# Self attention of a two-layer block: scores computed in both orientations, no transposed probabilities, the high parts of the exponentials made on ScalarE

## The chip, the cores and the metric

One core of a Trainium2 chip runs the whole program in one launch. The metric is device time in microseconds (us). The engines are TensorE (PE, with its weight loads PEld), VectorE (DVE), ScalarE (ACT), GpSimd (POOL) and SyncE (SP), which here only issues DMAs.

## The reference

The input x is 8 batches of 512 tokens with 512 features, the context 8 batches of 77 tokens with 384. Layer 0 is a cross attention and a feed-forward block, layer 1 a self attention, a cross attention and a feed-forward block. The change touches the self attention alone. In float32:

```python
xn = layernorm(x)                                   # eps 1e-5
q, k, v = (xn @ w.T + b).reshape(8, 512, 16, 32).transpose(0, 2, 1, 3)   # each with its own w, b
p = softmax(q @ k.T * 32 ** -0.5, axis=-1)          # 512 x 512 for each of 8 x 16 heads
x = x + (p @ v).transpose(0, 2, 1, 3).reshape(8, 512, 512) @ wo.T + bo
```

## The kernel before

The program runs five phases one after the other, with a barrier between them: L0ca, L0ff, L1sa, L1ca, L1ff. `self_attention` (line 525) is L1sa. Every matmul operand is split in two: a high part, rounded to the type fp32r, and a low part, what is left. A product takes three matmuls, high by high, low by high and high by low (`product`, line 88). High parts are made by ACT (`add_hi`, line 94), low parts by DVE (`add_lo`, line 100), those of the normalised tokens hT by POOL (`ln_lo`, line 231).

Per batch there are projections q and k in 4 groups of 4 heads each, V and the output O in 4 token tiles each (4 quarters each, a quarter is one `product` of 512 columns, 3 matmuls), and T, which transposes the normalised tokens (4 blocks of 4 transpositions). For the scores SP copies q and k into stacks (`stacks`, line 589): the 128 rows of the contraction hold the parts of one head as (high, high, low, low) of q against (high, low, high, low) of k, so one matmul gives the whole product (`scores`, line 700). A group takes 16 DMAs.

A batch is 64 steps v; a head is 4 of them. The order of the work is written out by hand in tables of steps (lines 575 to 580, `T_STEPS` and so on), the same on each engine. In step v, PE makes the scores of a tile six steps ahead, transposes four 128x128 blocks of normalised probabilities Pr (`P_transposed`, line 713) and multiplies V by the transposed probabilities of two steps before (`PV`, line 727; six matmuls of 256 columns). DVE takes the maxima of a score tile (line 934), ACT makes the exponentials with the negative maxima as bias and the row sums as a by-product (line 846), DVE inverts the sums (line 942), POOL multiplies (line 1060). ACT then makes the high part PTh of the transposed block and DVE the low part PTl. V is laid into zeroed blocks (`place_v`, line 1068) so that four heads fill the four quarters of one output bank.

```python
def body(b, last):
    for v in range(TILES):
        ...
        if ahead and v + LEAD != TILES:
            scores(*tile(b, v + LEAD))
        P_transposed(b, v)
        if v >= LAG:
            PV(b, v - LAG)
```

Each engine takes its instructions in order and waits at semaphores; a wait holds all that is queued behind it. A prologue loads the weights through four staging slots, which are the memory of Pr, splits them, normalises the tokens of batch 0 and computes q, k of group 0 and V.

## Time and profile before

| | us |
|---|---|
| median of 3 runs | 3689.26 (3686.32 to 3692.94) |
| the profiled execution | 3688.11, its span 3686.3 |
| PE busy | 3448.7 (94% of the span) |
| DVE, ACT, POOL busy | 1816.3, 1802.7, 1138.8 |
| self attention's window 1318 to 2412 | 1094, of it PE busy 1069.6 |

The span is the time from the first to the last instruction. A matmul's duration in the trace contains its way through the array, so two that follow each other overlap; what one costs is the distance of their starts. The same holds, less so, for ACT and DVE.

### The profile page before, as it was taken

What the parts mean: (1) busy time and instruction counts of PE and PEld (TensorE: products, weight loads), DVE (VectorE), ACT (ScalarE), POOL (GpSimd) and SP (SyncE); (2) the same over time, 40 slices, a digit from 0 to 9 for tenths busy, and PEclk for the clock granted to TensorE, in tenths of its full rate; (3) what the DMA queues carried; (4) which work ended last, traced back from release to release, by engine and by line L of the source; (5) the groups of instructions that cost most, each with busy time, mean ns of one, the idle gap of its engine ahead of it and who ended that gap; (6) DMA issues with size and microseconds to landing.
All of it is one profiled execution on the core that took longest, in us unless ns stands there. A gap on an engine that the chain in (4) does not pass through costs nothing. (4 is left out here: it accounts for less than half of the span.)

```text
span 3686.3 us, 51567 instructions
## 1 busy us (share of the span) xinstructions
PE 3448.7 (94%) x18384; PEld 2905.3 (79%) x18384; DVE 1816.3 (49%) x3472; ACT 1802.7 (49%) x4868; POOL 1138.8 (31%) x1576
## 2 busy tenths in 40 slices
PE   4899979999999799999999999977999989999999
PEld 3788858888888578888888888855888768888887
DVE  3566644222222277777777767745666442222221
ACT  2677634222222266666667667735667542222222
POOL 2455521111111134444434435414455311111110
PEclk8999989999999899999999999988999989999999
DMA  3112123111111232322322332321221131111010
GB/s 95 39 58 71 61 83 99 39 35 35 35 35 35 72 92 72 101 74 75 94 80 69 94 91 59 92 69 53 76 72 48 52 112 52 35 35 35 35 35 35
DMA packets 158341, 232.91 MB, mean 63 GB/s; under 512 B 35894, under 2 KB 53510, under 8 KB 158086
## 3 DMA queue, kind: packets, MB, share of 16 engines
q1 hardware_dynamic: 158086, 229.63, 20.7%
q8 instruction: 146, 2.39, 0.3%
q14 instruction: 109, 0.89, 0.1%
HBM read 115.45 MB, written 41.94 MB: 43 GB/s over the span
## 5 line engine op out<-in xcount | busy, mean ns | idle before, releaser
L1060 POOL TENSOR_SCALAR L1sa_Pr<-L1sa_Pr,L1sa_rinv 128x512 f32<-128x512 f32 x512 | 354.8, 702 | 595.7 <-DVE L1sa_rinv L942 595.7
L102 DVE TENSOR_TENSOR L1sa_PTl<-L1sa_t,L1sa_PTh 128x512 fp32r<-128x512 f32 x512 | 352.2, 688 | 193.2 <-ACT L1sa_PTh L96 183.5
L96 ACT ACTIVATE L1sa_PTh<-L1sa_t 128x512 fp32r<-128x512 f32 x512 | 305.6, 597 | 266.2 <-PE L1sa_o L91 251.2
L846 ACT ACTIVATE L1sa_Pr<-L1sa_s,L1sa_nmax 128x512 f32<-128x512 f32 x512 | 350.9, 685 | 77.8 <-DVE L1sa_nmax L934 72.3
L934 DVE TENSOR_REDUCE L1sa_nmax<-L1sa_s 128x1 f32<-128x512 f32 x512 | 346.9, 678 | 17.7 <-PE L1sa_s L709 17.7
L89 PE MATMUL L1sa_o<-L1sa_PTh,L1sa_Vbh 128*128 128x256 f32 x1024 | 330.4, 323 | 3.5 <-DVE L1sa_oTl L103 2.1
L422 DVE TENSOR_TENSOR L0ff_gl<-L0ff_gf,L0ff_gh 128x512 fp32r<-128x512 f32 x128 | 95.2, 743 | 475.3 <-ACT L0ff_gh L382 475.3
L422 DVE TENSOR_TENSOR L1ff_gl<-L1ff_gf,L1ff_gh 128x512 fp32r<-128x512 f32 x128 | 95.8, 749 | 473.1 <-ACT L1ff_gh L382 473.1
L723 PE MATMUL L1sa_t<-ident,L1sa_Pr 128*128 128x128 f32 x2048 | 312.2, 275 | 14.0 <-DVE L1sa_PTl L102 12.8
L723 PEld LDWEIGHTS L1sa_t<-ident,L1sa_Pr 128*128 128x128 f32 x2048 | 243.5, 141 | 92.8 <-DVE L1sa_PTl L102 24.5
L368 ACT ACTIVATE L0ff_gf<-L0ff_f,cols 128x512 f32<-128x512 f32 x128 | 88.3, 690 | 451.0 <-PE L0ff_f L91 451.0
L368 ACT ACTIVATE L1ff_gf<-L1ff_f,cols 128x512 f32<-128x512 f32 x128 | 88.3, 690 | 449.7 <-PE L1ff_f L91 449.7
L91 PE MATMUL L1sa_o<-L1sa_PTl,L1sa_Vbh 128*128 128x256 f32 x1024 | 288.9, 282 | 0.0
L90 PE MATMUL L1sa_o<-L1sa_PTh,L1sa_Vbl 128*128 128x256 f32 x1024 | 288.4, 282 | 0.0
L709 PE MATMUL L1sa_s<-L1sa_stack_k,L1sa_stack_q 128*128 128x512 f32 x512 | 205.2, 401 | 5.6 <-ACT L1sa_Pr L846 4.0
L89 PE MATMUL L0ff_f<-L0ff_hTh,L0ff_Wh 128*128 128x512 f32 x512 | 203.4, 397 | 5.7 <-POOL L0ff_hTl L232 5.7
L89 PE MATMUL L1ff_f<-L1ff_hTh,L1ff_Wh 128*128 128x512 f32 x512 | 202.9, 396 | 5.7 <-POOL L1ff_hTl L232 5.7
L89 PEld LDWEIGHTS L1sa_o<-L1sa_PTh,L1sa_Vbh 128*128 128x128 f32 x1024 | 194.8, 190 | 7.8 <-DVE L1sa_oTl L103 6.8
L90 PE MATMUL L0ff_f<-L0ff_hTh,L0ff_Wl 128*128 128x512 f32 x512 | 200.6, 392 | 0.0
L91 PE MATMUL L0ff_f<-L0ff_hTl,L0ff_Wh 128*128 128x512 f32 x512 | 200.5, 392 | 0.0
L90 PE MATMUL L1ff_f<-L1ff_hTh,L1ff_Wl 128*128 128x512 f32 x512 | 200.1, 391 | 0.0
L91 PE MATMUL L1ff_f<-L1ff_hTl,L1ff_Wh 128*128 128x512 f32 x512 | 200.0, 391 | 0.0
(296 smaller groups left out, 9380.3 us busy)
## 6 DMA issues: line engine op xcount, KB each, us to landing
L1sa_stack_q<-L1sa_parts_q SPq DMA_DIRECT2D x256, 128.0 KB, 2.7
L1sa_stack_k<-L1sa_parts_k SPq DMA_DIRECT2D x256, 128.0 KB, 2.7
L0ff_xs<-x SPq DMA_DIRECT2D x64, 256.0 KB, 3.5
L1sa_xs<-x SPq DMA_DIRECT2D x64, 256.0 KB, 3.5
L1ff_xs<-x SPq DMA_DIRECT2D x64, 256.0 KB, 3.5
L0ca_xs<-in_x SPq DMA_DIRECT2D x32, 256.0 KB, 3.6
L0ca_stage<-in_x SPq DMA_DIRECT2D x32, 256.0 KB, 3.9
x<-L0ca_stage SPq DMA_DIRECT2D x32, 256.0 KB, 2.0
```

The lines of the kernel that those rows point to most:

```text
L89: nc.tensor.matmul(out, wh, xh, start=first, stop=False)
L90: nc.tensor.matmul(out, wl, xh, start=False, stop=False)
L91: return nc.tensor.matmul(out, wh, xl, start=False, stop=last)
L96: return nc.scalar.activation(hi, bank, ACT.Copy)
L102: return nc.vector.tensor_tensor(lo, bank, f32(hi), ALU.subtract)
L368: nc.scalar.activation(gf[:, j % 2, :], f1_bank[j % 2][:, :], ACT.Gelu, bias=b1[:, j:j + 1])\
L422: nc.vector.tensor_tensor(gl[:, j % 2, :], gf[:, j % 2, :], f32(gh[:, j % 2, :]), ALU.subtract)\
L709: nc.tensor.matmul(s_bank[s % S_BANKS][:, :], stack["q"][:, g % 2, j, qt * P:(qt + 1) * P], stack["k"][:, g % 2, j, :], start=True, stop=T ...
L723: last = nc.tensor.transpose(t_bank[v % 2][:, (2 * k + q) * P:(2 * k + q + 1) * P], Pr[:, h % 2, qt, kt * P:(kt + 1) * P], cst.ident[:, :])
L846: nc.scalar.activation(Pr[:, h % 2, qt, :], s_bank[s % S_BANKS][:, :], ACT.Exp, bias=nmax[:, h % 2, qt:qt + 1], accum_out=rsum[:, h % 2, q ...
L934: nc.vector.reduce_max(nmax[:, h % 2, qt:qt + 1], s_bank[s % S_BANKS][:, :], AX.X, negate=True)\
L1060: nc.gpsimd.tensor_scalar(p, p, rinv[:, h % 2, qt:qt + 1], 0.0, ALU.mult, ALU.add)\
```

## The change

The self attention is rewritten; the other phases are as before.

- A step n is now a pair of tiles (32 steps a batch, 2 a head). The scores are taken in both orientations: query rows by key columns (`scores`), only for the maxima, and key rows by query columns (`scores_T`), for the exponentials. The stacks keep three of the four combinations of parts (96 rows), and two further rows hold the negative maxima, high and low, on q's side and ones on k's. So `scores_T` comes out with the maximum subtracted, and exp has no bias.
- The maxima (DVE) are split by POOL (`m_split`), transposed by PE into the first columns of the bank pair of `scores_T` (`m_transposed`), copied by ACT (`m_copy`) and put into the stack by a DMA (`m_rows`).
- exp writes E, 128x1024. ACT makes its high part Eh by a Copy (`e_hi`, for all steps: `EH_BY`), POOL in even and DVE in odd steps the low part El (`e_lo`). `PV` multiplies them with Vst, whose 96 columns are interleaved: V high, V low and ones, so that the sums come out as the third of three rows. It takes high and low in two halves of the step, 2 matmuls of 512 columns each.
- The result of a head, not normalised (96 rows), is copied out by ACT (`o_out`) and laid side by side by a DMA (`line_up`); per 4 heads POOL adds the two parts, DVE inverts 128x512 sums, POOL multiplies, ACT and DVE split.
- The projections are cut into quarters and spread evenly over the 64 half steps of a batch (`sa_pieces`). The order is q, k of group 2, O of the batch before, q, k of group 3, T, then q, k of group 0, V and q, k of group 1 of the next batch. `evacs[n]` are those whose bank is emptied in step n: T0 in step 15, T1, T2 and T3 in step 16.
- The weights come through three staging slots. The prologue also makes q and k of group 1.

```diff
+SA_ORDER = ([("q", 0, 2), ("k", 0, 2)] + [("O", -1, t) for t in range(TT)] + [("q", 0, 3), ("k", 0, 3)]
+            + [("T", 1, c) for c in range(KT)] + [("q", 1, 0), ("k", 1, 0)] + [("V", 1, t) for t in range(TT)]
+            + [("q", 1, 1), ("k", 1, 1)])
+SA_FIRST = [("T", c) for c in range(KT)] + [("q", 0), ("k", 0)] + [("V", t) for t in range(TT)] + [("q", 1), ("k", 1)]
+STEPS = H * 2
+def sa_pieces():
+    quarters = [(*u, c) for u in SA_ORDER for c in range(1 if u[0] == "T" else KT)]
+    halves = [[] for _ in range(2 * STEPS)]
+    for i, q in enumerate(quarters):
+        halves[i * 2 * STEPS // len(quarters)].append(q)
+    return halves
...
-        stack = {n: ph.sb(f"stack_{n}", [P, 2, 4, S], F32R) for n in "qk"}
+        KD, KM = 3 * HD, 3 * HD + 2
+        stack = {n: ph.sb(f"stack_{n}", [P, 8, S], F32R) for n in "qk"}
         parts = {n: ph.sb(f"parts_{n}", [P, 2, S], F32R) for n in "qk"}
-        Vh, Vl = (ph.sb(n, [P, TT, D], F32R) for n in ("Vh", "Vl"))
-        Vbh, Vbl = (ph.sb(n, [P, TT, 4, P], F32R) for n in ("Vbh", "Vbl"))
-        Pr = ph.sb("Pr", [P, 2, TT, S])
-        PTh, PTl = (ph.sb(n, [P, 2, S], F32R) for n in ("PTh", "PTl"))
-        nmax, rsum, rinv = (ph.sb(n, [P, 2, TT]) for n in ("nmax", "rsum", "rinv"))
+        V = ph.sb("V", [P, TT, 2, D], F32R)
+        VS = 5
+        Vst = ph.sb("Vst", [P, TT, VS, HD, 3], F32R)
+        E = ph.sb("E", [P, 2, 2 * S])
+        Eh, El = ph.sb("Eh", [P, 2, 2 * S], F32R), ph.sb("El", [P, 2, 2 * S], F32R)
+        nmax = ph.sb("nmax", [P, 2, TT])
+        mm = ph.sb("mm", [P, 2, 2 * TT], F32R)
+        mT = ph.sb("mT", [2 * TT, 2, P], F32R)
+        osb = ph.sb("osb", [3 * HD, S])
+        OLN = ph.sb("OLN", [P, 3, S])
+        onorm = x.htmp
...
-        wt = weight_staging(ph, [flat(Pr[:, i // 2, 2 * (i % 2):2 * (i % 2) + 2, :]) for i in range(4)])
+        wt = weight_staging(ph, [E[:, 0, :], E[:, 1, :], flat(OLN[:, 0:2, :])])
...
+        s_bank = ctx.enter_context(nc.psum_tensor(f"{name}_s", [P, 2, S], F32))
+        st_bank = ctx.enter_context(nc.psum_tensor(f"{name}_st", [P, 2, S], F32))
+        o_bank = ph.banks("o", 2)
...
+        LEAD_S, LEAD_T = 6, 2
...
+        EH_BY, EL_BY = ("act", "act", "act", "act"), ("pool", "dve", "pool", "dve")
...
+            def stacks(n, group, pair):
+                pset = 2 * group + pair
+                full = e_stack[pset % 4].sem
+                sp.wait_ge(e_qkl.sem, e_qkl.no(2 * group + "qk".index(n)))
+                if group >= 2:
+                    sp.wait_ge(e_st.sem, e_st.no(8 * (group - 2) + 4 * pair + 3))
+                for j in range(2 * pair, 2 * pair + 2):
+                    src = f32(parts[n][HD * j:HD * (j + 1), :, :])
+                    dst = f32(stack[n][:, 4 * (group % 2) + j, :])
+                    once, twice = (src[:, 0, :], src) if n == "k" else \
+                        (src[:, 1, :], src[:, 0:1, :].broadcast_to([HD, 2, S]))
+                    sp.dma_start(dst[0:2 * HD, :], twice).then_inc(full, 16)
+                    sp.dma_start(dst[2 * HD:3 * HD, :], once).then_inc(full, 16)
+            def m_rows(h):
+                sp.wait_ge(e_mc.sem, e_mc.no(h))
+                sp.dma_start(f32(stack["q"][KD:KM, h % 8, :].rearrange("a (t n) -> a t n", t=TT)),
+                             f32(mT[:, h % 2, :])).then_inc(e_m[h % 2].sem, 16)
+            def line_up(h):
+                sp.wait_ge(e_ob.sem, e_ob.no(h))
+                if h % 4 == 0 and h > 0:
+                    sp.wait_ge(e_on.sem, e_on.no(h // 4 - 1))
+                sp.dma_start(OLN[HD * (h % 4):HD * (h % 4 + 1), :, :],
+                             osb[:, :]).then_inc(e_oln.sem, e_oln.unit)
...
+                    if n % 2 and 0 <= (n + 3) // 2 < HEADS:
+                        m_rows((n + 3) // 2)
+                    if n % 2 == 0 and n >= 2:
+                        line_up((n - 2) // 2)
+                    if n < 0:
+                        continue
+                    for step, kind, ahead, g, pair in ((3, "q", 0, 2, 0), (5, "k", 0, 2, 0), (6, "q", 0, 2, 1),
+                                                       (6, "k", 0, 2, 1), (14, "q", 0, 3, 0), (14, "q", 0, 3, 1),
+                                                       (16, "k", 0, 3, 0), (16, "k", 0, 3, 1), (20, "q", 1, 0, 0),
+                                                       (22, "k", 1, 0, 0), (22, "q", 1, 0, 1), (22, "k", 1, 0, 1),
+                                                       (31, "q", 1, 1, 0), (31, "q", 1, 1, 1), (0, "k", 0, 1, 0),
+                                                       (0, "k", 0, 1, 1)):
+                        if step == s and exists(b + ahead) and not (b == 0 and s == 0):
+                            stacks(kind, (b + ahead) * G + g, pair)
...
+            def scores(n):
+                h, slot = n // 2, n // 2 % 8
+                if n % 4 == 0:
+                    pe.wait_ge(e_stack[n // 4 % 4].sem, e_stack[n // 4 % 4].no(n // 16))
+                if n > 0:
+                    pe.wait_ge(e_mx.sem, e_mx.no(n - 1))
+                for i in range(2):
+                    qt = 2 * (n % 2) + i
+                    last = nc.tensor.matmul(s_bank[:, i, :], stack["q"][0:KD, slot, qt * P:(qt + 1) * P],
+                                            stack["k"][0:KD, slot, :], start=True, stop=True)
+                last.then_inc(e_s.sem, e_s.unit)
+            def scores_T(n):
+                h, slot = n // 2, n // 2 % 8
+                if n % 2 == 0:
+                    pe.wait_ge(e_m[h % 2].sem, e_m[h % 2].no(h // 2))
+                if n % 2 and (n + 1) // 2 < HEADS:
+                    pe.wait_ge(e_mc.sem, e_mc.no((n + 1) // 2))
+                elif n > 0:
+                    pe.wait_ge(e_ex.sem, e_ex.no(n - 1))
+                for i in range(2):
+                    kt = 2 * (n % 2) + i
+                    last = nc.tensor.matmul(st_bank[:, i, :], stack["k"][0:KM, slot, kt * P:(kt + 1) * P],
+                                            stack["q"][0:KM, slot, :], start=True, stop=True)
+                last.then_inc(e_st.sem, e_st.unit)
+            def m_transposed(h):
+                pe.wait_ge(e_mm.sem, e_mm.at(h, 1))
+                if h > 0:
+                    pe.wait_ge(e_ex.sem, e_ex.no(2 * h - 2))
+                nc.tensor.transpose(st_bank[0:2 * TT, 0, 0:P], f32(mm[:, h % 2, :]), cst.ident[:, :])\
+                    .then_inc(e_mt.sem, e_mt.unit)
+            def PV(n, low):
+                h = n // 2
+                if low:
+                    by = EL_BY[n % 4]
...
+                for i in range(2):
+                    kt = 2 * (n % 2) + i
+                    last = nc.tensor.matmul(o_bank[h % 2][0:KD, :], flat(Vst[:, kt, h % VS, :, :]),
+                                            (El if low else Eh)[:, n % 2, i * S:(i + 1) * S],
+                                            start=n % 2 == 0 and not low and i == 0,
...
+                    if 0 <= n + LEAD_T < PAIRS:
+                        scores_T(n + LEAD_T)
+                    if n + LEAD_S < PAIRS:
+                        scores(n + LEAD_S)
+                    for half in range(2):
+                        if n >= 0:
+                            for kind, ahead, i, c in halves[2 * (n % STEPS) + half]:
+                                if exists(b + ahead):
+                                    piece(kind, b + ahead, i, c)
+                            PV(n, half == 1)
+                        if half == 0 and n % 2 == 0 and 0 <= n + 4 < PAIRS:
+                            m_transposed((n + 4) // 2)
...
+            def e_hi(n):
+                act.wait_ge(e_ex.sem, e_ex.no(n))
+                if n >= 2:
+                    act.wait_ge(e_pvh.sem, e_pvh.no(n - 2))
+                nc.scalar.activation(Eh[:, n % 2, :], E[:, n % 2, :], ACT.Copy).then_inc(e_eh["act"].sem, 1)
+            def exp(n):
+                act.wait_ge(e_st.sem, e_st.no(n))
+                if n < 2:
+                    act.wait_ge(wt.lo.sem, wt.lo.at(CHUNKS - 1, 0))
+                else:
+                    by = EL_BY[(n - 2) % 4]
+                    act.wait_ge(e_el[by].sem, e_el[by].no(kth(EL_BY, n - 2)))
+                nc.scalar.activation(E[:, n % 2, :], flat(st_bank[:, :, :]), ACT.Exp).then_inc(e_ex.sem, e_ex.unit)
+            def o_out(h):
+                act.wait_ge(e_pv.sem, e_pv.no(2 * h + 1))
+                if h > 0:
+                    act.wait_ge(e_oln.sem, e_oln.no(h - 1))
+                nc.scalar.activation(osb[:, :], o_bank[h % 2][0:KD, :], ACT.Copy).then_inc(e_ob.sem, e_ob.unit)
+            def m_copy(h):
+                act.wait_ge(e_mt.sem, e_mt.no(h))
+                if h >= 2:
+                    act.wait_ge(e_m[h % 2].sem, e_m[h % 2].no(h // 2 - 1))
+                nc.scalar.activation(mT[:, h % 2, :], st_bank[0:2 * TT, 0, 0:P], ACT.Copy)\
+                    .then_inc(e_mc.sem, e_mc.unit)
...
+                    if n % 8 == 3 and n >= 11:
+                        o_hi((n - 11) // 8)
+                    if n % 2 == 0 and n >= 2:
+                        o_out((n - 2) // 2)
+                    if 0 <= n + 1 < PAIRS and EH_BY[(n + 1) % 4] == "act":
+                        e_hi(n + 1)
+                    if 0 <= n + LEAD_T < PAIRS:
+                        exp(n + LEAD_T)
+                    if n >= 0:
+                        for kind, b_of, i in evacs[n]:
+                            if kind != "O":
+                                evacuate(kind, b_of, i)
+                    if n % 2 == 0 and 0 <= n + 4 < PAIRS:
+                        m_copy((n + 4) // 2)
...
+            def maximum(n):
+                h = n // 2
+                dve.wait_ge(e_s.sem, e_s.no(n))
+                nc.vector.reduce_max(nmax[:, h % 2, 2 * (n % 2):2 * (n % 2) + 2], s_bank[:, :, :], AX.X, negate=True)\
                     .then_inc(e_mx.sem, e_mx.unit)
+            def e_lo(n):
+                by = EH_BY[n % 4]
+                dve.wait_ge(e_eh[by].sem, e_eh[by].no(kth(EH_BY, n)))
+                if n >= 2:
+                    dve.wait_ge(e_pv.sem, e_pv.no(n - 2))
+                nc.vector.tensor_tensor(El[:, n % 2, :], E[:, n % 2, :], f32(Eh[:, n % 2, :]), ALU.subtract)\
+                    .then_inc(e_el["dve"].sem, 1)
...
+            def m_split(h):
+                pool.wait_ge(e_mx.sem, e_mx.no(2 * h + 1))
+                if h >= 2:
+                    pool.wait_ge(e_mt.sem, e_mt.no(h - 2))
+                nc.gpsimd.tensor_copy(mm[:, h % 2, 0:TT], nmax[:, h % 2, :]).then_inc(e_mm.sem, 1)
+                pool.wait_ge(e_mm.sem, e_mm.at(h, 0))
+                nc.gpsimd.tensor_tensor(mm[:, h % 2, TT:2 * TT], nmax[:, h % 2, :], f32(mm[:, h % 2, 0:TT]),
+                                        ALU.subtract).then_inc(e_mm.sem, 1)
+            def place_v(b, j):
+                h = b * H + j
+                if j == 0:
+                    pool.wait_ge(e_vl.sem, e_vl.no(b * TT + TT - 1))
+                if h >= VS:
+                    pool.wait_ge(e_pv.sem, e_pv.no(2 * (h - VS) + 1))
+                nc.gpsimd.tensor_copy(Vst[:, :, h % VS, :, 0:2].rearrange("p t d a -> p t a d"),
+                                      f32(V[:, :, :, HD * j:HD * (j + 1)])).then_inc(e_vst.sem, e_vst.unit)
```

In ACT's loop the order in a step is: o_hi, o_out, e_hi(n+1), exp(n+2), evacuations, m_copy. In DVE's: maximum(n+6), o_lo, e_lo(n+1), inverse, finishing of the evacuations, statistics and normalisation of the next batch (steps 9 to 14). In POOL's: e_lo(n+1), m_split, sum and scaling of a group, place_v, rsqrt, low parts of T, bias.

## Rows read from the trace of the kernel before

**Rows 1.** The page, part 1: busy time, share of the span, instructions.

```profile
PE 3448.7 (94%) x18384; PEld 2905.3 (79%) x18384; DVE 1816.3 (49%) x3472; ACT 1802.7 (49%) x4868; POOL 1138.8 (31%) x1576
```

**Rows 2.** Windows: length, busy time of PE, PEld, DVE, ACT, POOL, clock, DMA.

```profile
1318.00:2412.00 1094.00, 1069.60 (x7098) 935.57 (x7096) 812.45 (x1527) 745.16 (x1668) 497.50 (x830) 1.00 0.31 82
```

**Rows 3.** Tiles t and o: durations ns min/median/max, first and last start.

```profile
L723 PE MATMUL L1sa_t<-ident,L1sa_Pr x2048: 270/272/421, 1317.7 to 2416.8; 128*128 128x128 f32 x187
...
L91 PE MATMUL L1sa_o<-L1sa_PTl,L1sa_Vbh x1024: 274/283/290, 1323.6 to 2420.0; 128*128 128x256 f32 x171
```

**Rows 4.** Waits of weight loads, 1330 to 2430: us in total, times, longest.

```profile
PEld L1sa_t L723 <- DVE L1sa_PTl L102: 24.5, 47, 1.0
...
PEld L1sa_pj L89 <- POOL L1sa_hTl L232: 6.1, 7, 0.9
```

**Rows 5.** Timeline, 1350.3 to 1352: start us, duration us, what.

```profile
1350.33 0.39 PE L91 MATMUL L1sa_pj<-L1sa_hTl,L1sa_wqh 128*128 128x512 f32 x1
...
1350.56 0.40 PE L709 MATMUL L1sa_s<-L1sa_stack_k,L1sa_stack_q 128*128 128x512 f32 x1
...
1350.80 0.60 PE L723 MATMUL L1sa_t<-ident,L1sa_Pr 128*128 128x128 f32 x4
...
1351.15 0.36 PE L89 MATMUL L1sa_o<-L1sa_PTh,L1sa_Vbh 128*128 128x256 f32 x1
...
1351.95 0.39 PE L89 MATMUL L1sa_pj<-L1sa_hTh,L1sa_wkh 128*128 128x512 f32 x1
```

**Rows 6.** Timeline of ACT at three places, and the lines view of its Copy.

```profile
1295.07 1.99 ACT L143 ACTIVATE L1sa_wvh<-L1sa_Pr 128x1024 fp32r<-128x1024 f32 x2
...
1350.13 0.60 ACT L96 ACTIVATE L1sa_PTh<-L1sa_t 128x512 fp32r<-128x512 f32 x1 [0.82 <-PE L1sa_o L91]
...
1350.62 0.68 ACT L846 ACTIVATE L1sa_Pr<-L1sa_s,L1sa_nmax 128x512 f32<-128x512 f32 x1
...
L143 ACT ACTIVATE L1sa_wvh<-L1sa_Pr 128x1024 fp32r<-128x1024 f32 x2 | 2.0, 1046 | 0.0
```

**Rows 7.** Tiles stage and gl of L0ff: DVE with two SBUF inputs.

```profile
L148 DVE SCALAR_TENSOR_TENSOR L0ff_Wl<-L0ff_stage,L0ff_Wh x16: 1206/1226/2309, 534.5 to 623.1; 128x1024 fp32r<-128x1024 f32 x16
...
L422 DVE TENSOR_TENSOR L0ff_gl<-L0ff_gf,L0ff_gh x128: 691/693/1686, 551.3 to 1253.5; 128x512 fp32r<-128x512 f32 x128
```

**Rows 8.** Tile hTl: POOL's subtraction of 512 columns.

```profile
L232 POOL TENSOR_TENSOR L1sa_hTl<-L1sa_htmp,L1sa_hTh x32: 1258/1450/1452, 1280.4 to 2250.4; 128x512 fp32r<-128x512 f32 x32
```

**Rows 9.** Timeline of PE behind a gap of the prologue.

```profile
1298.56 0.79 PE L89 MATMUL L1sa_pj<-L1sa_wvh,L1sa_hTh 128*128 128x512 f32 x1 [4.12 <-DVE L1sa_wvl L148]
1299.15 0.63 PE L90 MATMUL L1sa_pj<-L1sa_wvh,L1sa_hTl 128*128 128x512 f32 x1
1299.58 0.63 PE L91 MATMUL L1sa_pj<-L1sa_wvl,L1sa_hTh 128*128 128x512 f32 x1
...
1301.61 0.39 PE L90 MATMUL L1sa_pj<-L1sa_wvh,L1sa_hTl 128*128 128x512 f32 x1
```

**Rows 10.** SP's timeline (one row), then DMAs: KB each, median us to landing.

```profile
1835.67 5.07 SPq L599 DMA_DIRECT2D L1sa_stack_q<-L1sa_parts_q  x8
...
L1sa_stack_q<-L1sa_parts_q SPq DMA_DIRECT2D x256, 128.0 KB, 2.7
...
L0ca_Kbh<-L0ca_Kh SPq DMA_DIRECT2D x32, 38.5 KB, 2.0
```

**Rows 11.** Timeline of the prologue, and landing of a weight load (last figure).

```profile
1275.40 2.35 DVE L148 SCALAR_TENSOR_TENSOR L1sa_wql<-L1sa_Pr,L1sa_wqh 128x1024 fp32r<-128x1024 f32 x2
...
1276.75 1.63 ACT L223 ACTIVATE L1sa_htmp<-L1sa_pj,cols 128x512 f32<-128x512 f32 x2 [2.13 <-PE L1sa_pj L218]
...
L1sa_Pr<-in_L_sa_wv SPq DMA_DIRECT2D x2, 512.0 KB, 4.2
```

**Rows 12.** Lines view: reciprocals of two and of four elements a partition.

```profile
L942 DVE RECIPROCAL L1sa_rinv<-L1sa_rsum 128x2 f32<-128x2 f32 x256 | 39.5, 154 | 0.6 <-ACT L1sa_Pr L846 0.6
...
L1657 DVE RECIPROCAL L0ca_rinv<-L0ca_rsum 128x4 f32<-128x4 f32 x128 | 20.9, 163 | 1.3 <-ACT L0ca_Pr L1583 1.2
```

799 lines of the change are left out of this document (308 added, 491 removed).

## The prediction, made before the changed kernel was run

> **What bounds the kernel now.** I read the page first: TensorE is busy 94% of the span [rows 1]. The change touches one stage, so I then read the windows of that stage: 1094 us in which PE is busy 1069.6, DVE 812, ACT 745, POOL 497 [rows 2]. PE paces it. The tile views give its loop: first transposition of probabilities at 1317.7, last PV product at 2420.0, so 1102.5 us [rows 3] for 8 batches x 16 heads, 8.6 us a head with the projections in it. The waits of PE in it are small (24.5 us on the low part of the probabilities, 6.1 on the low part of the normalised tokens) [rows 4]. The timeline has PE's prices by start-to-start times: a 512-column matmul 0.233 us, four transpositions 0.35, six 256-column PV matmuls 0.80 [rows 5].
>
> **PE, part by part.** Before, a step (v) is 0.235 + 0.35 + 0.80 = 1.385 us, 4 per head, 5.54 us. After, a head has 4 scores, 4 transposed scores and 8 PV matmuls, all of 512 columns: 16 x 0.233 = 3.73, and one small transposition of the maxima (0.12, one of the four above with its start). Gone: 16 transpositions and the third product of PV. The projections stay: 64 quarters (3 matmuls, 0.70 us) and 4 T blocks (0.35) a batch, so 2.80 + 0.09 a head. PE's own work falls from 5.54 + 2.89 = 8.43 to 6.74 us a head. Over 128 heads that is 216 us. If PE stayed the bound, that would be the gain.
>
> **The other engines.** A step after is two key tiles, two steps a head. ACT: a 128x1024 Copy lasts 1.046, two in 1.99, so it holds ACT for 0.945 [rows 6]. Exp over 1024 is not in the trace; Exp over 512 lasts 0.68, and a Copy over 1024 adds 0.45 to one over 512 (0.60): 0.68 + 0.45 = 1.13. Bounds: 1.046 (the Copy itself) and 2 x 0.68 = 1.36; I take 1.09, near the Copy, as both run at one rate over their elements. A 512 Copy out of PSUM holds ACT 0.49 (1350.13 to 1350.62). Per head 2 x (0.945 + 1.0) + 0.49 (o_out) + 0.25 (m_copy) = 4.6, with evacuations 5.4 of 6.7. DVE: maxima over 1024 twice and one e_lo of 1024, each 1.21 as the scalar-tensor-tensor (STT) of that size [rows 7]; with evacuations under 5.5. POOL: TENSOR_TENSOR over 512 lasts 1.26 to 1.45, so e_lo over 1024 between 2.5 and 2.9, I take 2.65 [rows 8]; with the sum and the scaling of a group of heads (1.35 each, a quarter of them a head), low parts and biases (8 x 1.35 a batch) 4.0, with m_split and place_v (three small ones, an estimate of 0.4 each, up to 1 if strides cost) 5.2. No engine is full. What decides is order.
>
> **The even step, laid out.** t = 0: PE starts scores_T(n+2). Then scores(n+6), a quarter, PV high: 0.47 + 0.47 + 0.70 + 0.47 = 2.10, where m_transposed stands. It overwrites the bank that exp(n+2) reads, so PE waits for that exp. ACT's queue has three instructions up to it: o_out, which needs the last PV of the step before (drained at 0.26), e_hi(n+1), exp(n+2): 0.26 + 0.49 + 0.945 + 1.09 + 0.05 = 2.84. PE stands 0.74 us, and behind it stand a quarter and PV low. A head takes 6.74 + 0.74 = 7.5 us. The rest fits: m_copy ends at 3.6, PE's next step starts at 4.2; POOL's e_lo of the next even pair runs 4.65 to 7.3 and is wanted by exp at 9.2; DVE's e_lo 2.2 to 3.4 is wanted at 4.9. Steps without quarters (4 heads in the first batch, 8 in the last) run on ACT's chain: exp(n+2) done at 2.84, the transposition and m_copy to 3.5, scores_T(n+3) to 4.1, its exp (behind e_hi) to 5.4, so about 5.5 a head (PE alone 3.85).
> Loop: 116 x 7.5 + 12 x 5.5 = 936 us.
>
> **Stalls once a batch (7 batches).**
> T block: T0 to T3 stand in steps 15 and 16 back to back, with q(1,0) right behind them; before they are at steps 35, 37, 39, 41. Three of the four evacuations fall into step 16 and htmp has two slots, so the chain T3 <- whole(1) (after o_out, e_hi, exp: 10.3 to 11.0, counted from step 14), hi(1) 11.8, lo(1) 13.2, whole(3) 14.0, lo(2) 15.2, hi(3) 15.8, lo(3) 17.2 (each the end of it) runs serially, with POOL at 1.35 and ACT at 0.78 each, while PE waits at q(1,0). Step 16 would end at 11.7 and ends at 17.25 + 0.70 + 0.47 = 18.4: 6.7 us. Then the clock: behind a 4.12 us gap PE's matmuls started 0.43 us apart, 1.2 GHz, from 1299.15 and 0.23 apart from 1301.61 [rows 9]: 3.05 us for seven starts that take 1.63 warm, so 1.4; I put 1.5 on it.
> SP's queue: eight stack DMAs hold SP 5.07 us, 0.6 each, and a small one lands in 2.0 [rows 10]. m_rows(h) must be issued between 3.6 of an even step and land before 7.5. In step 22 twelve stack DMAs stand ahead of it (1.3 to 8.5, landing 10.5): 3.0 us, of which the 0.74 is taken up, since ACT catches up meanwhile, so 2.2. In step 0 the eight k stacks wait for the evacuation of k(1,1) (4.2) and hold SP to 9.0; m_rows(2) lands at 11.1, and ACT's evacuation of q(0,2), queued ahead of e_hi(3) and exp(4), waits for the same stacks: 4.1. Step 6: 0.3. A third of the stack DMAs are of 64 KB; if those hold SP half as long, the three fall to about 4 together.
> O: o_lo is queued behind line-up, sum, inverse and scaling of the last group and stands 0.9 late for O(0) in step 3.
> Sum 6.7 + 1.5 + 2.2 + 4.1 + 0.3 + 0.9 = 15.7; x 7 = 110. The loop takes 936 + 110 = 1046 us, 56 less than now.
>
> **Ahead and behind.** Three staging slots in place of four: the second half of wk is loaded only after the first weight_lo (1276.6), lands 4.2 later, and ACT's weights_hi stand ahead of whole(0), which moves from 1276.75 to 1281.9 [rows 11]: 5.1. q(1), k(1) of batch 0 go ahead of the loop: 24 x 0.233 = 5.6. The ramp is serial: two scores with their maxima in one bank pair 3.5, split, transposition and copy 1.3, row DMA 2.1, scores_T(0) and exp(0) 1.8, transposition and copy of the next head, scores_T(1), exp(1) 2.7, 11.4 in all; now the first P_transposed (1317.7) starts 6.6 after V's last matmul (1311.1). Together 16. Behind: o_out 0.6, line-up DMA 2.7 [rows 10], inverse 1.7, scaling 1.4, then the same high and low parts and cold matmuls 1.5: 8.
> The reciprocal over 512: 154 ns for 2 elements and 163 for 4 [rows 12] give 4.5 ns each, 2.4 us; at an ordinary DVE rate it is 0.7. I take 1.7; off the path but for the tail.
> Sum: 1046 + 16 + 8 - 1102.5 = -32.5. The profiled execution took 3688.1 (span 3686.3), 1.2 under the median of 3689.3: 3688.1 - 32.5 = 3655.6, given as 3655.
>
> **A rule against it.** The 128x1024 STT on DVE goes from 1.21 to 2.31 and the gl subtraction from 0.69 to 1.69 [rows 7], both with two SBUF inputs. The Trainium skill (SBUF — State Buffer, on the shared port) says that DVE with two SBUF inputs and a GpSimd operation that reads SBUF exclude each other for a whole instruction. The trace agrees. By my layout the two e_lo lie apart (2.2 to 3.4 and 4.65 to 7.3); at a full collision e_lo on DVE would end near 4.9, just where exp wants it, so the sum stays. In the T block hi and lo collide, and that is in the 6.7.
> ScalarE: Activation LUTs (What ACT_TABLE_LOAD costs) gives 0.186 us + 0.833 ns an element with immediate scale and bias; by it Exp over 1024 would take 1.04 and the total would be 6 us less. No row has that shape.
>
> **Rivals.**
> (a) My case, ACT's chain in even steps and the stalls once a batch: 3655, from 3600 to 3700. Chance 0.48.
> (b) The stalls once a batch mostly aren't there (the row DMA lands early, the T chain overlaps). For it: SP was idle most of the time before. Against: 0.6 us a DMA is measured. 3655 less 60 to 90: about 3580. Chance 0.17.
> (c) PE stays full, no stall at m_transposed either: 116 x 6.74 + 12 x 5.5 = 848, and 3688.1 - 1102.5 + 848 + 24 = 3458. It needs ACT to finish three instructions in 2.1 us. Chance 0.06.
> (d) Slower. The three ACT instructions of an even step, each with its own wait, don't overlap at all and Exp takes its upper bound: 0.26 + 0.60 + 1.046 + 1.36 + 0.05 = 3.32 in place of 2.84, 116 x 0.48 = 56: 3711. For it: each has a wait in front, and Exp reads two banks. Against: Copy and Exp at 1350.13 and 1350.62 follow each other 0.49 apart though both wait too. It decides from 0.28 us a head, the 32.5 of gain over 116. Beyond 3735 it needs POOL too: an e_lo that ends after 9.2 (4.6 us long) holds back exp as well. Chance 0.29, of it 0.07 beyond 3735.
>
> **How the numbers follow.** Range: 3575 to 3735 leaves out (c), the 0.07 of (d) and 0.06 of (b), 0.19 together. A change under 0.2% (7 us) can't be told from none. Faster: (b), (c) and the part of (a) under 3682: 0.17 + 0.06 + 0.41 = 0.64; same, the rest of (a) and the lowest of (d), 0.09; slower 0.27.
>
> **What would show it.** PE waiting on ACT's Exp at the transposition of maxima, 128 times at 0.7 us; a wait of 5 us on hTl seven times, with a granted clock below 1 behind it; scores_T waiting for the row DMA in steps 22 and 0; PE busy for some 870 us of the loop; Exp 1024 at 1.09. Wrong, if those waits are absent (b, c), if Exp is over 1.3 us, or POOL's e_lo over 4 us (d).

## The result: 3765 us, slower by 2.1%

The changed kernel takes 3765.0 us (3762.1 to 3768.2 in four runs), the kernel before 3688.5 beside it (3686.3 to 3692.9): a ratio of 1.0206, 95% interval 1.0188 to 1.0224. The forecast was 3655 with a range of 3575 to 3735; the time is above the range.

The profiled execution has a span of 3760.3 us against 3686.3. Three stretches make up the 74.0 us between them. The loop runs from 1334.3 (scores_T of step 0) to 2479.5 (end of the last PV product), 1145.2 us against 1102.5 [rows 3]: +42.7, forecast -56. The prologue grew by 16.5, forecast 16. What lies behind the loop grew by 14.7, forecast 8. So the forecast was lost in the loop, 99 us of it.

The page of the changed kernel, part 1, answers to [rows 1]; under it the windows of its loop, to be read beside [rows 2] (length, then busy time of PE, PEld, DVE, ACT, POOL, granted clock, DMA share, GB/s):

```profile
PE 3321.8 (88%) x14928; PEld 2645.5 (70%) x14928; DVE 1751.4 (47%) x2608; ACT 1741.3 (46%) x4100; POOL 1233.9 (33%) x1384
...
1334.00:2480.00 1146.00, 936.47 (x3662) 673.42 (x3662) 742.22 (x669) 685.23 (x911) 592.70 (x642) 0.91 0.31 84
```

PE has 133 us less to do in the loop (936.5 for 1069.6) and the loop is longer. It stands for 210 us, where it stood for 24, and its mean clock in there is 0.91, where it was 1.00. Some of the 936 is itself that lower clock.

The same trace by instruction: the tile and lines views, durations in ns (min/median/max, or sum and mean). They answer to [rows 6, 8, 12]:

```profile
L856 ACT ACTIVATE L1sa_E<-L1sa_st x256: 995/1024/1031, 1330.0 to 2475.0; 128x1024 f32<-128x1024 f32 x128
...
L1040 POOL TENSOR_TENSOR L1sa_El<-L1sa_E,L1sa_Eh x128: 2346/2394/2413, 1332.8 to 2474.9; 128x1024 fp32r<-128x1024 f32 x128
L947 DVE TENSOR_TENSOR L1sa_El<-L1sa_E,L1sa_Eh x128: 1162/1217/1921, 1337.6 to 2477.5; 128x1024 fp32r<-128x1024 f32 x128
...
L952 DVE RECIPROCAL L1sa_OLN<-L1sa_OLN x32: 3341/3343/3354, 1370.4 to 2482.8; 128x512 f32<-128x512 f32 x32
```

The first three cost what the forecast gave them (1.217 for 1.21) or less. The reciprocal costs twice what I took, and lies above my upper bound.

The waits view from 1334 to 2480 (us in total, times, longest) stands in the place of [rows 4]:

```profile
PE L1sa_st L779 <- DMA L1sa_stack_q<-L1sa_mT: 98.6, 37, 5.0
PE L1sa_st L787 <- ACT L1sa_E L856: 44.3, 75, 1.5
ACT L1sa_parts_q L100 <- DMA L1sa_stack_k<-L1sa_parts_k: 36.4, 7, 5.2
PE L1sa_pj L92 <- POOL L1sa_hTl L235: 23.8, 7, 4.2
PE L1sa_pj L221 <- DVE L1sa_xs L215: 17.3, 7, 2.5
PE L1sa_pj L221 <- ACT L1sa_htmp L226: 11.8, 7, 1.8
PE L1sa_pj L92 <- DVE L1sa_oTl L106: 8.0, 7, 1.3
```

The largest wait by far is scores_T for the row DMA (L779 <- the copy of mT into the query stack), about 100 us. The stall the forecast laid out in every even step (L787, the transposition of maxima, waiting for the exponential) is there too. SyncE's timeline shows what holds the row DMA back, in steps 22 and 23 of the fourth batch (start us, duration us). The first row is ScalarE's copy of the maxima that the row DMA carries, the last four are PE's timeline, with the wait in brackets:

```profile
1877.81 0.27 ACT L868 ACTIVATE L1sa_mT<-L1sa_st 8x128 fp32r<-8x128 f32 x1
...
1875.53 0.61 SPq L652 DMA_DIRECT2D L1sa_OLN<-L1sa_osb  x1
1876.24 0.61 SPq L640 DMA_DIRECT2D L1sa_stack_k<-L1sa_parts_k  x1
1876.89 0.60 SPq L641 DMA_DIRECT2D L1sa_stack_k<-L1sa_parts_k  x1
...
1881.47 1.47 SPq L640 DMA_DIRECT2D L1sa_stack_k<-L1sa_parts_k  x1
...
1884.57 0.59 SPq L641 DMA_DIRECT2D L1sa_stack_k<-L1sa_parts_k  x1
1885.20 0.68 SPq L645 DMA_DIRECT2D L1sa_stack_q<-L1sa_mT  x1
...
1887.05 1.22 PE L779 MATMUL L1sa_st<-L1sa_stack_q,L1sa_stack_k 98*128 98x512 f32 x2 [4.85 <-DMA L1sa_stack_q<-L1sa_mT]
1888.06 1.05 PE L765 MATMUL L1sa_s<-L1sa_stack_k,L1sa_stack_q 96*128 96x512 f32 x2
1888.92 0.63 PE L92 MATMUL L1sa_pj<-L1sa_wvh,L1sa_hTh 128*128 128x512 f32 x1
1889.34 0.63 PE L93 MATMUL L1sa_pj<-L1sa_wvh,L1sa_hTl 128*128 128x512 f32 x1
```

Twelve stack DMAs run from 1876.24 to 1885.2, the row DMA is issued at 1885.20 and scores_T starts 1.85 later. Its data was ready at 1878.1, in step 22, so for seven microseconds it waited for nothing but its turn. Then PE's matmuls start 0.42 us apart and not 0.233. The windows view gives the clock they ran at, behind the wait and a few microseconds later:

```profile
1887.00:1890.90 3.90, 3.85 (x9) 3.08 (x10) 1.74 (x2) 1.49 (x2) 0.00 (x0) 0.50 0.17 50
1893.00:1900.00 7.00, 6.47 (x29) 4.77 (x29) 5.81 (x4) 4.51 (x7) 5.16 (x5) 1.00 0.00 1
```

A granted clock of 0.50 is the lower of the two levels, 1.2 GHz. Each long wait is paid once as a wait, and again in the step behind it, whose matmuls at the lower clock are called cold below.

### The profile page after: what moved, and what is told of

Same layout as the page of the kernel before. It is cut to its first block and busy times, and to the rows that moved or that the text cites. A ratio compares the mean times of both kernels' runs of the same rounds, so it can differ in the third digit from the quotient of the medians.

```text
span 3760.3 us, 43692 instructions
## 1 busy us (share of the span) xinstructions
PE 3321.8 (88%) x14928; PEld 2645.5 (70%) x14928; DVE 1751.4 (47%) x2608; ACT 1741.3 (46%) x4100; POOL 1233.9 (33%) x1384
## 5 line engine op out<-in xcount | busy, mean ns | idle before, releaser
L939 DVE TENSOR_REDUCE L1sa_nmax<-L1sa_s 128x2 f32<-128x1024 f32 x256 | 312.1, 1219 | 378.4 <-PE L1sa_s L765 377.4
L1040 POOL TENSOR_TENSOR L1sa_El<-L1sa_E,L1sa_Eh 128x1024 fp32r<-128x1024 f32 x128 | 306.0, 2391 | 431.1 <-ACT L1sa_Eh L847 359.5
L856 ACT ACTIVATE L1sa_E<-L1sa_st 128x1024 f32<-128x1024 f32 x256 | 260.4, 1017 | 130.5 <-PE L1sa_st L779 128.6
L779 PE MATMUL L1sa_st<-L1sa_stack_q,L1sa_stack_k 98*128 98x512 f32 x512 | 180.8, 437 | 101.8 <-DMA L1sa_stack_q<-L1sa_mT 100.9
L847 ACT ACTIVATE L1sa_Eh<-L1sa_E 128x1024 fp32r<-128x1024 f32 x256 | 267.4, 1045 | 0.2
L779 PEld LDWEIGHTS L1sa_st<-L1sa_stack_q,L1sa_stack_k 98*128 98x128 f32 x512 | 101.8, 208 | 151.5 <-DMA L1sa_stack_q<-L1sa_mT 121.3
L94 PE MATMUL L1ff_acc<-L1ff_Wl,L1ff_gh 128*128 128x512 f32 x512 | 199.3, 389 | 0.0
L94 PE MATMUL L0ff_acc<-L0ff_Wl,L0ff_gh 128*128 128x512 f32 x512 | 199.3, 389 | 0.0
L92 PE MATMUL L0ff_acc<-L0ff_Wh,L0ff_gh 128*128 128x512 f32 x512 | 199.2, 389 | 0.0
L93 PE MATMUL L0ff_acc<-L0ff_Wh,L0ff_gl 128*128 128x512 f32 x512 | 199.2, 389 | 0.0
L92 PE MATMUL L1ff_acc<-L1ff_Wh,L1ff_gh 128*128 128x512 f32 x512 | 199.2, 389 | 0.0
L93 PE MATMUL L1ff_acc<-L1ff_Wh,L1ff_gl 128*128 128x512 f32 x512 | 199.2, 389 | 0.0
```

The lines of the kernel that those rows point to most:

```text
L92: nc.tensor.matmul(out, wh, xh, start=first, stop=False)
L93: nc.tensor.matmul(out, wl, xh, start=False, stop=False)
L94: return nc.tensor.matmul(out, wh, xl, start=False, stop=last)
L779: last = nc.tensor.matmul(st_bank[:, i, :], stack["k"][0:KM, slot, kt * P:(kt + 1) * P], stack["q"][0:KM, slot, :], start=True, stop=True)
L847: nc.scalar.activation(Eh[:, n % 2, :], E[:, n % 2, :], ACT.Copy).then_inc(e_eh["act"].sem, 1)
L856: nc.scalar.activation(E[:, n % 2, :], flat(st_bank[:, :, :]), ACT.Exp).then_inc(e_ex.sem, e_ex.unit)
```

## Where the time of a batch goes

A step is counted from one first scores_T matmul to the next in PE's timeline. Undisturbed steps take 4.06 (even) and 3.25 us (odd), 7.31 a head, where I forecast 7.5. This table has the third batch of every kernel that ran. The column 14 stands for an undisturbed even step; the last is the whole batch of 32.

```
step             1     2     3     7     8    11    14    15    16    17    19    20    23    24   batch
after         7.07  6.35  4.63  5.05  4.18  3.86  4.06  7.05 10.91  4.55  5.09  3.47  8.20  6.11   146.9
rows_act      3.25  9.04  5.13  3.25  4.06  3.51  4.06  4.40 10.84  3.91  3.25  4.06  3.26  4.07   132.7
sp_spread     4.49  8.51  4.97  3.25  4.06  3.72  4.06  6.86 10.85  4.43  5.45  3.46  3.25  4.07   137.9
fill          7.09  4.26  5.24  5.06  4.16  5.19  4.06  6.23 10.85  4.44  5.64  3.46  7.80  4.05   143.6
act_order     7.08  5.03  4.62  7.90  6.26  4.56  3.36  7.72 10.60  4.70  5.75  6.35 10.53  5.69   151.2
both          3.24  8.64  5.13  3.25  4.07  8.79  3.36  7.74 10.54  4.58  3.26  3.66  3.37  4.05   136.5
both_noinv    3.24  8.63  5.14  3.25  4.07  4.34  3.36  7.99 10.55  4.59  3.25  3.64  3.36  4.05   132.1
after_noinv   7.07  5.01  5.25  5.06  5.72  3.25  4.07  7.04 10.92  4.58  3.75  3.56  8.27  6.67   146.8
early         3.24  4.08  7.87  3.25  4.07  4.74  3.36  7.90 11.35  3.61  3.26  3.91  3.36  4.05   131.1
early_t       3.24  4.30  8.78  3.25  4.07  4.24  3.36  7.89  3.55  2.72  7.62  4.82  3.25  4.05   131.2
rows_early8   3.24  4.07  7.06  3.25  4.07  3.49  4.06  4.41 10.82  4.48  3.25  4.06  3.25  4.06   132.1
early8        3.24  3.63  7.73  3.25  4.07  4.38  3.36  7.57 10.53  4.50  3.26  3.67  3.38  4.04   129.7
early8_o      3.24  4.18  4.52  3.25  4.06  4.20  3.36  7.89 11.36  3.83  3.26  3.90  3.36  4.04   129.6
```

Sixteen heads of 7.31 are 117.0, so 29.9 us of the changed kernel's batch are stalls; the forecast had 15.7. Steps 1, 2, 7, 8, 19, 20, 23 and 24 hold some 16 of them (row DMA and the cold matmuls behind it), steps 15 to 17 hold 12 (T blocks), step 3 holds 1.4 (O).

## The experiments

**The row DMA leaves SyncE's queue (rows_act).**

```
-  SyncE, odd n:   m_rows((n + 3) // 2)
+  ScalarE, even n, behind m_copy((n + 4) // 2):   m_rows((n + 4) // 2)     # nc.scalar.dma_start
```

> Edit: the row DMA (the eight rows of negated maxima's halves that scores_T needs) is issued by ScalarE right after its copy of the transposed maxima; SyncE keeps all other DMAs in their order. Theory A (what costs is SyncE's queue: the row DMA stands behind up to twelve stack DMAs of 0.6 us each): PE's waits for it in steps 7, 19 and 23 go, with the cold matmuls of step 24: 1.8 + 2.0 + 5.0 + 2.0 = 10.8 us a batch. In steps 1 and 2 most of the wait stays, since scores(n+6) of step 2 needs the k stacks that land there at the same time; 1 us goes. 7 x 11.8 = 83, and 6 in the last batch, so 3765 - 89 = 3676. Theory B (the row DMA lands late because the DMA engines are busy with the stacks' bytes, whichever queue issues it): under 20 us of gain, 3745 to 3765. If issuing costs ScalarE 0.6 us a head beside what it has, it stays within its slack (5.4 of 7.3 us a head).

3655.4 us, ratio to the kernel before 0.9918 (0.9890 to 0.9947): 110 us less than the change, 83 to 89 expected from theory A. Steps 7, 8, 19, 20, 23 and 24 are undisturbed, though the stacks move the same bytes beside it. So it was the place in the queue, and theory B falls. Not all of the 110 us is the queue: step 15 fell too, by 2.65 us in each of seven batches (19 us), for a reason that the experiment both shows below. That leaves 91 us beside the 83 to 89. Issuing takes about as long on ScalarE, and the undisturbed steps stay at 4.06 and 3.25. The tile view:

```profile
L866 ACTq DMA_DIRECT2D L1sa_stack_q<-L1sa_mT x128: 620/621/1240, 1327.3 to 2358.5; - x128
```

As expected, the turn of the batch kept most of its loss (steps 1 to 3 together 17.4 for 18.1). Its form surprised me. The waits view shows ScalarE's evacuation of q waiting for the k stacks of step 0, as in the change; PE then waits for the exponential queued behind that evacuation (longest 3.9 us):

```profile
PE L1sa_st L780 <- ACT L1sa_E L849: 82.7, 97, 3.9
ACT L1sa_parts_q L100 <- DMA L1sa_stack_k<-L1sa_parts_k: 34.7, 7, 5.1
```

The stalls of its batch are 132.7 - 117.0 = 15.7 us, and its time is 3655: both are the forecast's numbers, and both by chance. Its T blocks cost 8.6 us and its batch turn 6.9, where the forecast had 8.2 and 5.0, with 2.5 for the steps that are now clean.

The Trainium skill (DMA: Bandwidth & Descriptors, Rules for kernel authors) says that spreading DMAs over issuing engines doesn't help the bandwidth and only saves the sequencer's issue time. No run here measures the bandwidth side. The issue time, and the order in it, was worth some 90 us of this kernel.

**SyncE's bursts broken up (sp_spread).**

```
-  (6,"q",0,2,1), (6,"k",0,2,1), (14,"q",0,3,0), (14,"q",0,3,1), (16,"k",0,3,0), (16,"k",0,3,1),
-  (20,"q",1,0,0), (22,"k",1,0,0), (22,"q",1,0,1), (22,"k",1,0,1), ... (0,"k",0,1,0), (0,"k",0,1,1)
+  (6,"q",0,2,1), (7,"k",0,2,1), (14,"q",0,3,0), (15,"q",0,3,1), (16,"k",0,3,0), (17,"k",0,3,1),
+  (20,"q",1,0,0), (21,"k",1,0,0), (22,"q",1,0,1), (23,"k",1,0,1), ... (0,"k",0,1,0), (1,"k",0,1,1)
```

> Edit: SyncE's stack DMAs are put one call (4 DMAs) a step where two or three stood in steps 6, 14, 16 and 22: 6 and 7, 14 and 15, 16 and 17, 20 to 23; the last call of step 0 goes behind the row DMA of step 1. The same DMAs, the same bytes, the same queue. Theory A (queue order): the row DMA stands behind at most four of 0.6 us: the waits of steps 7 and 23 go with the cold clock of step 24 (1.8 + 5.0 + 2.0 = 8.8 us a batch); in steps 1 and 2 what is won at scores_T is lost again at scores(n+6), which wants the last stack; 7 x 8.8 = 62: 3703. Theory B (traffic of the DMA engines, or the landing itself): nothing or under 15 us, 3750 to 3765.

3697.0 us, ratio 1.0027 (1.0011 to 1.0044): 68 us less than the change, 62 expected. Same queue, same DMAs, only their order among the row DMAs. Steps 7, 8, 23 and 24 are clean; step 1 gained 2.6 and step 2 lost 2.2. Step 19 stays (5.45), where four loads of residuals stand in front of the row DMA, in this run as in the change, whose rows these are:

```profile
1862.69 2.03 SPq L671 DMA_DIRECT2D L1sa_xs<-x  x4
1864.77 0.67 SPq L645 DMA_DIRECT2D L1sa_stack_q<-L1sa_mT  x1
```

**PE kept busy in front of the wait (fill).**

```
+  if n % STEPS in {2: 14, 24: 20} and n > 2 and b + 1 < B:
+      filler(n + LEAD_S - 1, count)      # count matmuls of 512 columns into the bank of the maxima
   scores_T(n + LEAD_T)
```

> Edit: ahead of scores_T in steps 2 and 24 of each of seven batches, where PE waits 3.8 and 5.0 us for the row DMA, PE repeats 14 and 20 matmuls (128 rows, 512 columns, 0.233 us each: 3.3 and 4.7 us) into the bank of the maxima, which scores(n+6) overwrites afterwards; it computes nothing new. Theory A (the slow steps 2 and 24, 6.3 and 5.2 us in place of 4.06 and 3.25, are the granted clock dropped because PE stood): both steps return to their warm lengths, the waits for the row DMA shrink to under 0.5 and 0.3 us, and 4.2 x 7 = 29 us go: 3736. Rival (those matmuls are slow for another reason, such as the stacks' DMA traffic into SBUF, or the clock is pulled down by the density of the stage): no gain, 3765 or a little more.

3745.3 us, ratio 1.0162 (1.0122 to 1.0202): 20 us less than the change for matmuls that compute nothing; 29 expected. (The 5.2 and 3.25 for step 24 in the expectation are a slip: it is an even step, 6.1 against 4.07.) Steps 2 and 24 are back at 4.26 and 4.05. The fill stands in six steps 2 (not in the first batch) and in seven steps 24; these thirteen steps are 25 us shorter together, and some of it comes back in step 3 (5.24 for 4.63). The timeline of step 24 of the fourth batch (start us, duration us) with the fill, against the one of the change above, and the windows row of the same step:

```profile
1875.16 0.73 PE L787 MATMUL L1sa_st<-L1sa_stack_q,L1sa_stack_k 98*128 98x512 f32 x2 [0.66 <-DMA L1sa_stack_q<-L1sa_mT]
1875.73 0.63 PE L765 MATMUL L1sa_s<-L1sa_stack_k,L1sa_stack_q 96*128 96x512 f32 x2
1876.19 0.40 PE L92 MATMUL L1sa_pj<-L1sa_wvh,L1sa_hTh 128*128 128x512 f32 x1
1876.43 0.39 PE L93 MATMUL L1sa_pj<-L1sa_wvh,L1sa_hTl 128*128 128x512 f32 x1
...
1875.10:1879.00 3.90, 3.84 (x17) 3.01 (x18) 2.61 (x3) 2.27 (x4) 0.00 (x0) 1.00 0.17 50
```

The granted clock is 1.00 where it was 0.50, at the same DMA share of 0.17. So the clock theory holds, and the rival, traffic of the stack DMAs, falls.

**The stall of the even steps (act_order).**

```
-  if n % 2 == 0 and n >= 2: o_out((n - 2) // 2)
   e_hi(n + 1)
   exp(n + LEAD_T)
+  if n % 2 == 0 and n >= 2: o_out((n - 2) // 2)
```

> Edit: ScalarE takes the finished head's output out of PSUM (o_out) behind the exponential in place of ahead of the high part. Theory A (the 0.69 us stall at the transposition of maxima is ScalarE's chain of three: o_out, high part, exp): the chain is 0.50 shorter and no longer waits for the last PV product, so exp ends at 2.0 to 2.1 of the even step, where PE arrives at 2.10; even step 4.06 to 3.4, 0.66 x 112 = 74 us: 3691. Rival (the exponential is held by something else, POOL's low part of 2.39 us for the same buffer, or the chain is only moved to the next step): less than half of it, 3730 to 3765.

3793.0 us, ratio 1.0291 (1.0262 to 1.0321): 28 us slower than the change, where 74 faster was expected. Even steps did fall from 4.06 to 3.36, as theory A had it to the tenth. But steps 7, 8, 20 and 23 of the third batch grew by 2.1 to 2.9 each (step 20 in four of the seven batches). The shorter steps want their row DMAs sooner while SyncE's list takes as long as before, and line_up, which stands in that list, waits for an output that now leaves PSUM after the exponential: in step 22 it is issued 2.2 us into the step, where in the change it was 0.8. From the waits view of its loop:

```profile
PE L1sa_st L779 <- DMA L1sa_stack_q<-L1sa_mT: 148.8, 42, 7.4
PE L1sa_st L787 <- ACT L1sa_E L856: 6.1, 13, 1.7
```

The wait of L787 went (44.3 to 6.1) and the one of L779 took it and more (98.6 to 148.8). Neither of my two theories had named this.

**Both edits together (both).** The edit is that of rows_act and act_order.

> Edit: the two edits rows_act and act_order together. With act_order alone even steps fell from 4.06 to 3.36 us but the waits for the row DMA grew by as much and more, as line_up then holds SyncE longer. Theory A (the even step's gain is real, and was eaten by the row DMA's place in SyncE's queue): with the row DMA on ScalarE nothing is left to eat it; rows_act's 3655 less 0.69 us x 100 even steps = 3586, less a little if ScalarE, which now issues the row DMA in its chain, falls late (even steps 3.4 to 3.6). Rival (ScalarE is the bound by then: its work of 5.4 us and 0.6 for the DMA a head against a head of 6.6, in the wrong order): even steps of 3.8 or more, 3630 to 3655.

3676.7 us, ratio 0.9973 (0.9961 to 0.9984): 21 us slower than rows_act, where 69 faster was expected. Theory A falls as stated, and so does the rival: ScalarE's even steps are 3.36. The table has the loss in steps 11 (+5.3), 15 (+3.3) and 17. VectorE's timeline around step 10 (the last bracket is the idle time in front and what ended it):

```profile
1780.50 3.35 DVE L951 RECIPROCAL L1sa_OLN<-L1sa_OLN 128x512 f32<-128x512 f32 x1 [2.45 <-DMA L1sa_OLN<-L1sa_osb]
1783.77 0.63 DVE L244 TENSOR_TENSOR L1sa_xs<-L1sa_pj,L1sa_xs 128x512 f32<-128x512 f32 x1
1784.32 0.68 DVE L195 BATCH_NORM_STATS2 L1sa_stats<-L1sa_xs 128x6 f32<-128x512 f32 x1
1784.91 1.21 DVE L938 TENSOR_REDUCE L1sa_nmax<-L1sa_s 128x2 f32<-128x1024 f32 x1
```

VectorE stands 2.45 us for the line-up, is held 3.35 by the reciprocal, and only then takes the maximum that frees the bank for scores(n+6). For step 15 the same engine's normalisation of the next tokens, four instructions, first in both, then in rows_act, each with POOL's row beside it:

```profile
1801.72 4.25 DVE L215 TENSOR_SCALAR L1sa_xs<-L1sa_xs,L1sa_mv,L1sa_rs 128x512 f32<-128x512 f32 x4
...
1802.88 2.35 POOL L1039 TENSOR_TENSOR L1sa_El<-L1sa_E,L1sa_Eh 128x1024 fp32r<-128x1024 f32 x1 [0.68 <-ACT L1sa_Eh L840]
```

```profile
1788.27 2.11 DVE L215 TENSOR_SCALAR L1sa_xs<-L1sa_xs,L1sa_mv,L1sa_rs 128x512 f32<-128x512 f32 x4
...
1790.12 2.48 POOL L1039 TENSOR_TENSOR L1sa_El<-L1sa_E,L1sa_Eh 128x1024 fp32r<-128x1024 f32 x1 [1.38 <-ACT L1sa_Eh L840]
```

In both, POOL's low part starts at 1802.88 while the four run, and they take 4.25 us together; in rows_act they take 2.11, and POOL starts within the last one. The Trainium skill (SBUF — State Buffer, Who interferes with whom) gives GpSimd and some VectorE instructions a shared pair of ports that is held for a whole instruction. The 4.25 against 2.11 agrees. The change itself has the same overlap, with PE behind it:

```profile
1835.62 4.03 DVE L215 TENSOR_SCALAR L1sa_xs<-L1sa_xs,L1sa_mv,L1sa_rs 128x512 f32<-128x512 f32 x4
...
1836.55 2.36 POOL L1040 TENSOR_TENSOR L1sa_El<-L1sa_E,L1sa_Eh 128x1024 fp32r<-128x1024 f32 x1 [1.84 <-ACT L1sa_Eh L847]
...
1839.79 0.97 PE L221 MATMUL L1sa_pj<-ident,L1sa_xs 128*128 128x128 f32 x4 [2.48 <-DVE L1sa_xs L215]
```

One by one, three of the four take 0.53 us and the third 2.66; it ends 0.3 behind POOL's instruction. In eleven of the thirteen kernels of the table POOL's low part starts before the last of the four, in all seven batches, and one of them then takes 2.56 to 2.69 us. In rows_act and rows_early8 it starts within the last one, and none takes over 0.76; these two alone have a step 15 of 4.4. No run took the overlap away by itself, so it is read from traces and not tested.

**The reciprocal left out (both_noinv, after_noinv).** Both kernels leave out most of the normalisation by the sum.

```
-  nc.vector.reciprocal(OLN[:, 2, :], OLN[:, 2, :])
+  nc.vector.reciprocal(OLN[:, 2, 0:4], OLN[:, 2, 0:4])
```

> Edit: both, with VectorE's reciprocal of the sums (128x512, 32 times) cut to 4 columns, so most of the normalisation by the sum is left out; every event and every other instruction stays. Theory C (both lost what its shorter even steps gave because VectorE's queue has the 3.34 us reciprocal, behind a wait for the line-up DMA, ahead of the maximum that scores(n+6) waits for: 3.4 us and cold matmuls in step 11, more in step 3): step 11 falls from 9.0 to under 4.5 us, step 3 by about 1: 5.5 x 8 = 44 and perhaps 7 more, 3677 - 50 = 3627. Rival D (the wait is for the line-up DMA, which comes late whatever the reciprocal costs): 1 us of the 5.5, under 15 us in all: over 3660. Rival E (ScalarE's chain paces the steps): no change, 3677.

3638.8 us, ratio 0.9875 (0.9855 to 0.9894): 38 us less than both, theory C's 50 not quite reached, D and E out. Step 11 fell from 8.8 to 4.3; step 3 did not move. The waits view of the loop, first of both, then of both_noinv with the line of its reciprocal, now 173 ns long. PE's wait for the maximum fell from 21.6 to 3.3 us, and VectorE waits for the line-up as before (the last row):

```profile
PE L1sa_s L758 <- DVE L1sa_nmax L938: 21.6, 8, 4.1
```

```profile
PE L1sa_s L758 <- DVE L1sa_nmax L938: 3.3, 4, 1.0
...
L951 DVE RECIPROCAL L1sa_OLN<-L1sa_OLN 128x4 f32<-128x4 f32 x32 | 5.5, 173 | 25.2 <-DMA L1sa_OLN<-L1sa_osb 25.0
```

> Edit: the change as it is, with the reciprocal cut to 4 columns in the same way (most of the normalisation by the sum is left out). It measures what the mis-sized term (3.34 us in place of the 1.7 of the forecast) costs in the change itself. Theory C: the wait for the low part of the normalised output in step 3 (1.3 us, and its share of the cold matmuls) goes, step 11 loses 0.5: 7 x 1.8 + 1.6 in the tail = 14 us: 3751. Rival (nothing waits for it in the change, since the row DMA is what is late there): 3765. Rival (VectorE's queue is behind the waits at the T blocks too): over 30 us, below 3735.

3750.8 us, ratio 1.0179 (1.0158 to 1.0199): 14 us less, the number of theory C, but not by its way. The wait for O in step 3 did not go (it is 1.9 us now, behind a shorter step 2), so the reciprocal wasn't what it stood for. From the third batch on the sum of a batch is the same, 146.8: steps 2, 11 and 19 fell by 3.3 together, steps 3, 8, 20 and 24 rose by 2.8, and PE meets the row DMA of step 23 where it did. The 14 us are 4.5 and 3.0 in the first two batches and the rest in the last batch and the tail. So in the change the mis-sized reciprocal is a small item; it only became the bound once the larger one was gone.

**The stacks of the batch turn issued early (early), and the T blocks apart (early_t).** On top of both:

```
+  if i >= at + 16: half = 45 + (i - at - 16) * 15 // 20      # last 20 quarters end in step 29, not 31
   stack calls one a step; second group: (29,"q",1,1,0), (30,"q",1,1,1), (31,"k",1,1,0), (31,"k",1,1,1)
early_t besides:
+  if at <= i < at + KT: half = (30, 31, 33, 34)[i - at]       # T blocks
+  elif at + KT <= i < at + 16: half = 39 + (i - at - KT) // 2 # first product of the new tokens: step 19
   four stack calls one or two steps later; POOL's scaling of one group a batch waits for the last low part of T
```

> Edit: on top of both: the last 20 quarters of the projections of the next batch stand in steps 22 to 29 in place of 22 to 31, so that the stacks of its second group of heads are issued in steps 29 to 31 and not in steps 31 and 0; the other stack calls stand one a step. Theory A (what is left in steps 1 to 3, 5.5 us and 2 to 3 of cold matmuls behind it in every batch, is ScalarE and PE waiting for the k stacks that SyncE can only issue in step 0): steps 2 and 3 return to about 3.4 and 3.3 with 1.3 to 2 left for the low part of the normalised output in step 3; 6 us x 7 = 42 below both, about 3545 if both comes at 3586. Rival (the wait at the batch turn is for ScalarE's own chain or the projections, and comes back in steps 29 to 31): under 15 us.

3650.4 us, ratio 0.9900 (0.9880 to 0.9919): 26 us less than both, 42 expected, and not where it was expected. Step 2 fell by 4.6; step 3 rose by 2.7, where PE now meets the reciprocal of the last group (1.5 us for the maximum, 2.6 for the low part of the normalised output), which the later wait had covered. Steps 2 to 4 together lost 0.9 us a batch on average over the second to seventh, so the rival is right about the batch turn. The gain is step 11, 4.2 us a batch in the same six, and by the traces it comes from the other half of the edit: with one stack call a step SyncE issues the line_up of step 8 2.9 to 3.5 us into that step, in both 4.8 to 6.6, and the reciprocal stands 0.5 us for it, not 2.4.

> Edit: on top of early: the four T blocks stand in steps 15, 15, 16 and 17 with the first projection of the new tokens in step 19, not all within steps 15 and 16 with the projection right behind them. Theory A (the 6.8 us of step 16 is the serial chain of copy, high part and low part of the T blocks with two buffers, in front of which PE stands): the wait for the low part of the normalised tokens goes and steps 15 to 18 together lose about 6 us a batch: 7 x 6 = 42, about 3505 if early comes at 3545. Rival (PE has too little other work in those steps, so ScalarE's and GpSimd's chain paces them as long): under 15 us.

3648.4 us, ratio 0.9896 (0.9879 to 0.9912): no gain over early, where 42 us was expected; the rival holds. Step 16 fell from 11.35 to 3.55, but step 19 rose from 3.26 to 7.62 and steps 20 and 21 from 3.91 and 3.25 to 4.82 and 4.64. The likely reason is that the projections that were to fill steps 16 to 18 wait for the same tokens and come in a lump behind; the run also moved stack calls and POOL's scaling, which it doesn't separate. Moving the T blocks' wait is not removing it.

**What is left, and the fastest version (early8, rows_early8, early8_o).**

```
-  store at (6, 8, 9, 11), then load at (7, 9, 10, 12)
+  load at (8, 9, 10, 12), then store at (6, 8, 9, 11)      # early8 on top of early
rows_early8: the same, with ScalarE's order of the change
early8_o, on top of early8:
+  if 8 <= i < 24: half = 9 + (i - 8) * 13 // 16               # output projection from step 4 on
```

> Edit: early (ScalarE's output copy behind the exponential, rows on ScalarE, early stacks), with only the first load moved from step 7 to 8, behind the line-up. Theory D (in early, VectorE stood 2.4 us at the reciprocal for the line-up of head 3, which SyncE issued behind a load that waits for a store to land; in steps 11 and later this is PE's wait for the maximum): step 11 falls from 4.7 (8.0 in batch 0) to 3.7, and 8 to 15 us go in all: 3640. Theory C (the reciprocal's own 3.34 us): under 4 us of change, 3650. Rival: the load is now late for the statistics of step 9, and step 15 grows from 7.9: slower than 3655.

3638.0 us, ratio 0.9872 (0.9853 to 0.9892): 12 us less than early, theory D's number, from two runs that lie 10 us apart. Step 11 fell by 3.5 us in the first batch and by 0.4 to 0.7 in the six others, to 4.2 to 4.4 and not to 3.7.

> Edit: rows_act, with the last 20 projection quarters in steps 22 to 29, the stack calls one a step (the second group's in steps 29 to 31), and SyncE's first load of the next tokens in step 8 in place of 7, behind the line-up, since there it waits for a store to land. ScalarE's order stays as in the change. Theory A+C (the row DMA, the k stacks of step 0 and the line-up behind the load are what is left beside the T blocks and the 0.69 us of every even step): steps 2 and 3 fall from 8.9 and 5.3 to about 4.1 and 5.0, 5 us x 7 = 35, step 11 by 0.5: 3655 - 38 = 3617. Rival (the batch turn is paced by VectorE's reciprocal and maxima, as it was in early, and keeps 3 us of the 5): 3640.

3642.9 us, ratio 0.9887 (0.9871 to 0.9904), nearer to the rival's 3640 than to 3617: step 2 is clean, and step 3 took 1.9 of its 5.0 us back.

> Edit: early8, with the 16 quarters of the output projection in halves 9 to 21 of a batch in place of 7 to 21, so that the first stands in step 4 and not in step 3. Theory (what is left at the batch turn in early8 is PE in front of the first output quarter, waiting for the low part behind the 3.35 us reciprocal, 2.75 us and cold matmuls behind it): step 3 falls from 7.9 by 2.5 to 3.5 us, one us of it comes back as denser steps 4 to 10 whose even ones are at PE's own pace: 2 to 3 us x 7 = 14 to 20, 3638 - 17 = 3621. Rival (the 1.7 us in front of scores in step 3, the maximum behind the reciprocal, then stands for longer, or ScalarE's chain takes it): under 7 us, 3631 to 3640.

3628.5 us, ratio 0.9839 (0.9823 to 0.9856): 9.5 us less than early8, between theory and rival. Step 3 fell by 3.2 us, as the theory had it, and steps 4 and 6 took 2.1 back. This version is faster than both kernels, 1.6% under the one before and 3.6% under the change, with the change's own instructions in another order and the row DMA issued by ScalarE.

## Why the prediction failed, step by step

- **PE's own work and the even step.** Right. The stall at the transposition of maxima makes an even step 0.7 us longer (4.06 for the 3.36 of act_order) against 0.74, a head takes 7.31 us against 7.5, ScalarE's Exp 1.02 against 1.09. A head without projections that nothing else held took 5.39 against 5.5. Rival (d), the one I gave for slower, did not happen: o_out, high part and exponential start 0.50 and 0.94 us apart, as in [rows 6].
- **SyncE's queue, the failed step.** The term "2.2, 4.1 and 0.3" made 6.6 us a batch and measures 16.2 (steps 1 and 2 6.1, 7 and 8 1.9, 19 and 20 1.2, 23 and 24 7.0). The mechanism was named, with its place, and the runs bear it out: two edits of the queue alone, rows_act and sp_spread, took some 91 and 68 us away. In step 0 even the landing was right: 11.1 us forecast, 11.15 measured. Four things were sized wrong. (1) In step 22 the twelve DMAs take 9.0 us, not 7.2: they are 0.635 apart, one lasts 1.47, and line_up is ahead of them. (2) I let the 0.74 of the even step be taken up by the wait; the row DMA was due at 7.3, landed at 12.3, and PE waited all 5.0. (3) The low clock behind these waits cost 2.3 us in step 2 and 2.0 in step 24, and the one cold start I priced, 1.5 us, was put behind the T blocks alone, though [rows 9] stood for any long gap. (4) Step 19, where four residual loads (2.0 us) stand in front of the row DMA, wasn't in the count at all (1.2 us with step 20), and step 6 to 8 is 1.9 for 0.3. My escape, that 64 KB DMAs might hold SyncE half as long, is wrong: they hold it 0.6 us as the 128 KB ones do.
- **T block.** 6.7 + 1.5 forecast, 11.9 measured. The chain of copies is there (3.4 us wait for hTl, 1.7 for htmp), but PE is already 2.5 us late at T0 for the normalised tokens (L221 <- xs), a wait that I hadn't laid out. Under "A rule against it" I asked of the two e_lo and of the T block whether VectorE and GpSimd hold each other up, but not of the four normalising instructions of step 14, where the traces show it. In rows_act, where it is absent, the T blocks take 8.6. early_t shows that placing alone doesn't recover it.
- **O** 0.9, measured 1.4.
- **The sum.** 14.2 us a batch too little in seven batches is 99 us: 67 of it SyncE's queue, 26 the T blocks, 3 the output projection, the rest small. That this equals what the loop missed is chance. The heads were 0.19 us too dear, 22 us the other way; the last batch took 121 us where 104 were forecast, with 15 us of waits for the row DMA in it (up to 4.1 us), and the first two batches had 4 us more of stalls.
- **Reciprocal.** Taken at 1.7 (bound 2.4), measured 3.34: 6.5 ns for each of 512 elements. With the 173 ns of the reciprocal of 4 columns it is 6.2 ns an element over some 0.15 us; the 4.5 that I drew from two and four elements [rows 12] rests on a difference of 9 ns. It was off the path of the change but for the last batch and the tail (14.7 for 8) and 7.5 us in the first two batches, as after_noinv shows.
- **Rival (b)**, no stalls once a batch, doubted the term that failed, but in one direction only. What I should have written as the slower rival is the row DMA's stall at double the price plus a cold start of 1.5 behind each of the two long waits: 7 x (6.6 + 3.0) = 67 us more, 3722. By itself it stays within the range; the T blocks and the last batch carry the time beyond it.

Left open: what the T chain costs at least, and whether the long normalisation in front of step 15 is POOL's overlap alone, as the thirteen traces suggest.

## What to carry to other kernels

When a step gets a small DMA on its path, write out everything ahead of it in its queue for every step of the period, not for the two worst, and then give it a queue of its own before anything else is tuned. An edit that shortens a step must be judged with the next queue in mind: here 0.7 us off each even step made the kernel slower twice, first behind SyncE's DMAs, then behind VectorE's reciprocal. Add the cold matmuls behind a long PE wait to its price: here the waits of 3.7 and 4.8 us cost 2.3 and 2.0 more.

## What was not expected of the hardware

- The issue of a DMA holds SyncE about 0.6 us (median) at 64, 128 and 192 KB alike, and 0.66 for the 4 KB one; ScalarE 0.62.
- A reciprocal over 128x512 float32 takes 3.34 us on VectorE, where the subtraction of twice that many elements takes 1.22.
- Fourteen and twenty idle matmuls, 3.3 and 4.7 us of PE's work in the place of waits, made a kernel 20 us faster; the granted clock behind the wait was 1.00 and not 0.50.
- A TENSOR_SCALAR of VectorE that takes 0.53 us took 2.56 to 2.69 when it began with GpSimd's subtraction of 2.4 us or up to 0.34 us behind its start, in 77 of 77 cases; one that was some 0.3 us under way by then kept its 0.53 (rows_act, rows_early8).
